# Retention stage: the decays clipped by two relus on ScalarE, the product with the norm's gain on GpSimd

## What is computed

```python
x_ln = layernorm(x)
beta = clip(sigmoid(x_ln @ Wbeta.T + bbeta), 0.85, 0.9995)   # 32 heads, 2 decays each
mix = softmax(x_ln @ Wmix.T + bmix)                          # over the 2 decays
# q, k rotated; phi = elu(.) + 1
def step(carry, xs):
    K = K * bt + pk
    S = S * bt + pk * vt
    num, den = pq . S, pq . K + EPS
    y = sum(num / den * mt)                                  # over the 2 decays
y = ys @ Wout.T + bout
z = x_ln + y
x = x + (z - mean(z)) / sqrt(var(z) + 1e-5) * ln_g + ln_b
```

## Time and profile before

| | us |
|---|---|
| median of 3 runs | 2272.37 |
| lowest, highest | 2271.41, 2273.75 |
| profiled execution, its own time | 2265.08 |
| its span, first to last instruction | 2263.4 |
| VectorE busy, whole span | 1702.2 (75%) |
| ScalarE busy | 1016.5 (45%) |
| GpSimd busy | 498.3 (22%) |
| TensorE busy | 1980.8 (88%) |

### The profile page before, as it was taken

How to read it: one execution, slowest core, us unless ns; L and a number is a source line. 1 busy time by engine, 2 the same in 40 slices (tenths; PEclk the granted TensorE clock), 3 DMA queues, 4 the chain that set the end, 5 groups by cost and what they waited for, 6 DMA issues and landing times. The chain is left out here.

```text
span 2263.4 us, 35922 instructions
## 1 busy us (share of the span) xinstructions
PE 1980.8 (88%) x12434; PEld 1484.5 (66%) x12434; DVE 1702.2 (75%) x5243; ACT 1016.5 (45%) x1596; POOL 498.3 (22%) x560
## 2 busy tenths in 40 slices
PE   5786799987999867754699978999999999979999
PEld 3554699976999823322699965566556555549998
DVE  6997788865888769999588876766766766628887
ACT  3442244433444333322344444566665665554443
POOL 1110100012000023221100014534533544230000
PEclk8998899998999987776799989999999999989999
DMA  3000100000000000000000000000000000000000
GB/s 97 6 5 4 54 1 1 1 1 1 1 1 2 13 27 1 0 1 0 1 1 1 1 1 1 1 1 1 1 1 1 1 1 1 1 1 6 11 11 15
DMA packets 17638, 15.75 MB, mean 7 GB/s; under 512 B 4209, under 2 KB 16177, under 8 KB 16946
## 3 DMA queue, kind: packets, MB, share of 16 engines
q1 hardware_dynamic: 15152, 12.66, 1.8%
q10 hardware_dynamic: 2306, 0.78, 0.2%
HBM read 10.55 MB, written 2.88 MB: 6 GB/s over the span
## 5 line engine op out<-in xcount | busy, mean ns | idle before, releaser
L2256 DVE TENSOR_REDUCE soft_mx<-psum 128x1 f32<-128x512 f32 (+3 forms) x608 | 380.4, 659 | 198.5 <-PE psum L2127 111.9
L2173 ACT ACTIVATE soft_prob<-psum 128x1024 f32<-128x1024 f32 (+3 forms) x384 | 305.1, 813 | 209.8 <-PE psum L2054 208.9
L2123 PE MATMUL psum<-soft_own,soft_stack 128*128 128x512 f32 (+3 forms) x768 | 250.4, 376 | 18.9 <-DVE soft_mx L2256 16.5
L2054 PE MATMUL psum<-soft_stack,soft_own 128*128 128x512 f32 (+3 forms) x768 | 228.4, 381 | 2.9 <-POOL soft_stack L2029 2.2
L2054 PEld LDWEIGHTS psum<-soft_stack,soft_own 128*128 128x128 f32 x768 | 121.2, 189 | 134.1 <-issue 74.7
L2123 PEld LDWEIGHTS psum<-soft_own,soft_stack 128*128 128x128 f32 x768 | 139.2, 191 | 77.7 <-DVE soft_mx L2256 63.1
L2071 PE MATMUL psum<-soft_prob,soft_v_pad 128*32 128x512 f32 (+3 forms) x1536 | 163.9, 498 | 3.5 <-ACT soft_prob L2173 2.1
L1056 DVE SCALAR_TENSOR_TENSOR x<-psum,ffn1b_cw,x 128x128 f32<-128x128 f32 x512 | 144.0, 343 | 30.1 <-PE psum L934 21.3
L1056 DVE SCALAR_TENSOR_TENSOR x<-psum,ffn0b_cw,x 128x128 f32<-128x128 f32 x512 | 144.1, 343 | 29.9 <-PE psum L934 21.5
L1056 DVE SCALAR_TENSOR_TENSOR x<-psum,ffn1a_cw,x 128x128 f32<-128x128 f32 x512 | 144.1, 344 | 29.8 <-PE psum L934 21.0
L1056 DVE SCALAR_TENSOR_TENSOR x<-psum,ffn0a_cw,x 128x128 f32<-128x128 f32 x512 | 144.1, 344 | 29.5 <-PE psum L934 21.0
(11 more groups left out here) (435 smaller groups left out, 3845.4 us busy)
## 6 DMA issues: line engine op xcount, KB each, us to landing
s_ffn_w<-in_ffn_w SPq DMA_DIRECT2D x4, 1024.0 KB, 8.3
out_x<-x SPq DMA_DIRECT2D x8, 256.0 KB, 2.3
x<-in_x SPq DMA_DIRECT2D x4, 384.0 KB, 7.4
mamba_coef_dram<-mamba_out_coef SPq DMA_DIRECT2D x8, 96.0 KB, 1.6
s_ret_w<-in_ret_w SPq DMA_DIRECT2D x1, 640.0 KB, 3.5
x<-in_x SPq DMA_DIRECT2D x4, 128.0 KB, 3.9
s_ret_cos<-in_ret_cos SPq DMA_DIRECT2D x1, 512.0 KB, 4.9
s_ret_sin<-in_ret_sin SPq DMA_DIRECT2D x1, 512.0 KB, 5.5
```

Source lines behind the costliest of these rows:

```text
L2054: ins = pe.matmul(e_ps[:, n % 2, j, low(n):BLK], own[:, u % 3, 2 * pair + j, kt * P:(kt + 1) * P], stack[:, u % HT, qb * BLK + low(n):(qb ...
L2123: ins = pe.matmul(per_head[:, n, :], stack[:, u % HT, i * P:(i + 1) * P], own[:, u % 3, g, half * BLK:half * BLK + width], start=(n == 0), ...
L2173: nc.scalar.activation(prob[:, done % PROBS, :, low(n):BLK], e_ps[:, n % 2, :, low(n):BLK], ACT.Exp, scale=float(HD) ** -0.5).then_inc(exp ...
L2256: nc.vector.tensor_reduce(mx[:, i, half, heads.start:heads.stop], bank[:, 0:width * len(heads)].rearrange("p (g k) -> p g k", k=width), AX ...
```

## The change

`beta` is clipped on ScalarE. With t for the tanh, relu(0.5 t + (0.5 - 0.85)), then relu(-that + (0.9995 - 0.85)), then -that + 0.9995 gives clip(0.5 t + 0.5, 0.85, 0.9995). The three biases are columns of a new tile `clip`, set by three memsets on VectorE at the stage's start. The three steps take the place of L1583, each waiting for the one before it; the clip on VectorE (L1683) goes. The product `zn` * `ln_g` goes from VectorE's `finish` (L1751) to a new GpSimd step `gain`, behind `keep` in GpSimd's order; x += zn stays on VectorE.

```diff
+            def gain(q):
+                pool.wait_ge(zn_ready, q + 1)
+                nc.gpsimd.tensor_tensor(zn[:, :, :], zn[:, :, :], w["ln_g"][:, :].unsqueeze(1).to_broadcast([P, GT, P]),
+                                        ALU.mult).then_inc(gained, 1)
...
                 if i + 2 < BLOCKS:
                     keep(i + 2)
+                if i:
+                    gain(i - 1)
             z_power(BLOCKS - 1)
+            gain(BLOCKS - 1)
...
+            act.wait_ge(clip_ready, 3)
...
-                nc.scalar.activation(beta[:, a % 2, :, :], th[:, :, :], ACT.Identity, bias=w["half"][:, :], scale=0.5)\
-                    .then_inc(beta_ready, 1)
+                now = beta[:, a % 2, :, :]
+                nc.scalar.activation(now, th[:, :, :], ACT.Relu, bias=clip[:, 0:1], scale=0.5).then_inc(beta_ready, 1)
+                act.wait_ge(beta_ready, a + 1)
+                nc.scalar.activation(now, now, ACT.Relu, bias=clip[:, 1:2], scale=-1.0).then_inc(narrowed, 1)
+                act.wait_ge(narrowed, a + 1)
+                nc.scalar.activation(now, now, ACT.Identity, bias=clip[:, 2:3], scale=-1.0).then_inc(clipped, 1)
...
+            for i, bias in enumerate((0.5 - BETA_MIN, BETA_MAX - BETA_MIN, BETA_MAX)):
+                nc.vector.memset(clip[:, i:i + 1], bias).then_inc(clip_ready, 1)
...
             def features(a):
                 p = a % 2
-                dve.wait_ge(beta_ready, a + 1)
-                nc.vector.tensor_scalar(beta[:, p, :, :], beta[:, p, :, :], BETA_MIN, BETA_MAX, ALU.max, ALU.min)\
-                    .then_inc(clipped, 1)
                 dve.wait_ge(exp_done, a + 1)
...
             def finish(q):
-                dve.wait_ge(zn_ready, q + 1)
-                nc.vector.tensor_tensor(zn[:, :, :], zn[:, :, :], w["ln_g"][:, :].unsqueeze(1).to_broadcast([P, GT, P]),
-                                        ALU.mult).then_inc(gained, 1)
                 dve.wait_ge(gained, q + 1)
```

More of the change, by code:

```diff
@@ L1363, in retention_stage @@
         eps = sb("eps", [P, 1])
+        clip = sb("clip", [P, 3])
         shift = sb("shift", [P, GT])
@@ L1389, in retention_stage @@
         ring_ready, ring_used, tanh_done = sem("ring_ready"), sem("ring_used"), sem("tanh_done")
-        beta_ready, clipped = sem("beta_ready"), sem("clipped")
+        beta_ready, narrowed, clipped, clip_ready = sem("beta_ready"), sem("narrowed"), sem("clipped"), sem("clip_ready")
         mix_ps_ready, mix_tanh_done, mix_ready = sem("mix_ps_ready"), sem("mix_tanh_done"), sem("mix_ready")
```

## The result

The changed kernel takes 2278.49 us (median of 7 runs, 2276.05 to 2281.42); the kernel before took 2271.41 (median of 7 runs, the three known ahead of the prediction among them). The ratio is 1.0033, with a 95% interval of 1.0022 to 1.0045: slower, by some 7 us (5 to 10 by that interval). The profiled execution has a span of 2276.0 us instead of 2263.4.

What follows compares the result with a forecast made beforehand. VectorE, busy 32.62 of a block's 33.20 us, was taken as the bound. Start +4.9, i = 1 to 5 +3.7, i = 6 -0.3, i = 7 +0.3, end +0.65 gave +9.2 us: 2281.6 us, range 2273.5 to 2286.

Steps and rivals of the forecast that it cites:

- Start, two blocks: Blocks 0 and 1: two more ScalarE activations delay `phi` by 2.36 us each, plus 0.15 for memsets; +4.9 us.
- Later blocks on ScalarE: Middle blocks: ScalarE's 2.36 us longer chain stays covered, with three us to spare; cost 0.
- The clip goes, the gain goes: VectorE in each middle block: it saves 0.60 us for the clip and 0.71 us for the gain.
- The power of z held by `phi`: GpSimd in middle blocks: `phi` stretches it to about 1.9 us, so `keep` starts 1.1 us behind `kv`, not 0.1.
- What comes back: Scans of i = 1 to 5: `keep` and gain now collide with them, +2.06 us against -1.31, net +0.75 a block.
- i = 6, i = 7, the end: Last blocks: no `keep` in i = 6, -0.3 us; no clip in i = 7, +0.3; last gain alone, +0.65.
- GpSimd goes on in one run: Rival, middle blocks: three GpSimd instructions run without letting a scan in, +2.0 us, so 2283.6; chance 0.10.
- `keep` stays covered: Rival, middle blocks: `keep` still falls under `kv` and only the gain collides; +4.3 us, so 2276.7; chance 0.12.
- VectorE gets its full saving: Rival, middle blocks: scans never wait for GpSimd, so the change gives -3.0 us, 2269.4; chance 0.10.
- the rule beside the rows: VectorE and GpSimd's shared port as a full-duration lock: 1.27 us for each of 12 collisions, not 1.04; 2284.4.

Runs made afterwards that it cites:

- e4: The whole change, but blocks 0 and 1 clipped on VectorE as before; stage 307.25 us against the change's 311.54, ratio to the kernel before 1.0017.
- e1: The kernel before with only the clip moved to ScalarE, the gain product staying on VectorE; stage 309.36 us against 303.70, ratio 1.0022.
- e3: The whole change with `keep` ahead of the power of z in GpSimd's order; stage 307.32 us against the change's 311.54, ratio to the kernel before 1.0024.
- e7: The kernel before plus one unused 128x512 GpSimd product per block, where the change has its gain; stage 310.29 us against 303.70, ratio 1.0025.
- e10: e6 without the wait that holds the gain back, so the gain runs beside scans again; stage 297.19 us, ratio to the kernel before 0.9973.
- e8: As e7 but with the unused GpSimd product at 128x256; stage 306.65 us against 303.70 in the kernel before, ratio 1.0016.
- e6: e3 and e4 combined, the gain held back to run beside the reciprocal, x += zn behind invert, last gain on VectorE; 2258.19 us, ratio to the kernel before 0.9951.
- e9: e6 with the gain product back on VectorE, together with x += zn behind invert; stage 293.74 us, ratio to the kernel before 0.9956.
- e2: The kernel before with only the gain product moved to GpSimd, the clip staying on VectorE; stage 303.89 us against 303.70, ratio 1.0008.

## Why the prediction was right

Sign, mechanism and order of the terms held; the size was a little too large, 2281.6 against 2278.49, +9.2 against +7.84 in the stage. The time lies 0.5 us below the stretch from 2279 to 2284 that the prediction gave to its forecast alone, so it is the rows and the experiments, not the time, that tell the forecast from its rivals. By its steps:

- *Start, two blocks* (+4.9): right. 2.36, 2.35 and 0.16; the exp as the last thing waited for; e4 gives it back.
- *Later blocks on ScalarE* (0): right. No wait for `ret_ex` or `ret_beta` behind block 1.
- *The clip goes, the gain goes* (-0.60, -0.71): right, 3.61 in six and 5.04 in seven.
- *The power of z held by `phi`* (`keep` 1.1 us behind the start of `kv` instead of 0.1): right, 1.92 us and 1.07; `keep` slides out. e1 and e3 show that this sliding out is what the clip's move costs in the middle. One reading was incomplete: alone the power takes 1.01 us, so the 1.39 of before was already a delay. In all three cases it ends 0.8 to 0.9 us behind the end of the VectorE instruction during which it started: the clip before, `phi` after, a scan in the earlier trace rows. So the clip, with one input, seems to have held it too, and being held by VectorE is then not a matter of two inputs alone; no run tests the clip by itself.
- *What comes back* (+2.06 a block): mis-sized. The scans of block 1 lose (2.37 + 5.74) - (1.42 + 4.78) = 1.91, the others 1.84 to 1.94. The term that failed is the 0.15 us that the first scan was to wait for L1433 on top of two meetings. L1434 ended 875.15 where the scan was wanted at 875.08, and what came of that was a turn, not an extra wait. Five blocks make 0.8 us of it. From `phi` of i = 1 to `phi` of i = 2 it is 33.98 us, where 34.2 was expected and 33.46 stood before.
- *i = 6, i = 7, the end* (-0.3, +0.3, +0.65): the end was 0.62; the scans lose 1.02 in block 6 and 0.96 in block 7, where 1.04 each was expected.
- Left out altogether: `ym`'s small wait for the spread (0.2 us in some blocks), which gets shorter when the gain no longer stands in front of invert: about -0.25.
- Of the 3.1 us between 2281.6 and 2278.49 the stage is 1.4. Another 1.0 is in the basis: over seven runs before gave 2271.41, where I had added to the 2272.37 of three. The last 0.8 us no run explains.

Of the rivals, *GpSimd goes on in one run* was half true: in blocks 1, 3 and 5 L1434 and L1436 ran without a scan between them, in 2 and 4 they did not. The total was nearly the same (1.91 to 1.94 and 1.84 to 1.85), so here it is the number of meetings that counts, not who comes first. *`keep` stays covered* fell with e1; *VectorE gets its full saving* with e7 and e10.

On the rule beside the rows: in the Trainium skill, "SBUF — State Buffer", section "SBUF: two separate sides", the lock is held for the whole instruction. e7 and e8 show a scan blocked for all but 0.24 to 0.30 us of a GpSimd instruction, at two sizes: the trace agrees in kind, and the duration is shorter than the rule's. e6 shows a reciprocal with one input not blocked at all. Why 0.3 us are free is open: no run here tests it.

## What to carry to other kernels

When two engines block each other without a semaphore, no wait shows it: look for instructions of one engine that are longer than their like, and for what the other engine did at that moment. An instruction taken off the bound engine moves everything behind it, and so moves other engines' work out from under the instructions that it was hidden by; ask of each neighbour what it will lie beside afterwards. A wait that gets shorter does the same, as e9 shows. And place moved work by what it will run beside: the same product on GpSimd cost 1.0 us a block among scans and nothing beside a reciprocal.

## What I had not expected of the hardware

- A scan is blocked for GpSimd's duration less about 0.30 us, at 128x512 (1.26 us, 0.96 lost) and 128x256 (0.72 us, 0.42 lost); a scan that carries no state in, for that duration less 0.24.
- A four-element GpSimd instruction (the power of z, 1.01 us alone) took 1.39 us when it started under the clip and 1.92 under `phi`, while `phi` kept its 1.22 us beside it both times.
- Which engine has the turn when both ask within 0.1 us alternated from block to block in the changed kernel, and the total changed by 0.1 us at most. GpSimd went on in blocks 1, 3 and 5, whose scans carry a state in, and the scan went first in 2 and 4, whose scans carry none; whether that decides it, no run tests.
- The granted clock of TensorE over the last 16 projections was at the lower level for most of that work in some kernels (0.56 before) and full in others (1.00 in e2), which makes 1.5 us of the stage. TensorE had in both cases worked on the spread and then waited for `ym`. Four kernels (e2, e6, e9, e10) had 3.42 us from `ym` to z and the other eight 4.84 to 5.16; what decides it is open, so comparisons of the stage across these two sets carry it, and I have taken it out where I say so.
